# A two-layer transformer on one core: the retention layer laid out transposed, value weights centred once, gate by batch, head variance by a selector product, and a new order of all steps

## The chip, the cores and the metric

One core of a Trainium2 chip runs the whole program in one launch. The metric is the time on the device in microseconds, the median of three executions. TensorE (PE; its weight loads are shown as PEld) multiplies matrices, VectorE (DVE) and ScalarE (ACT) work on vectors and can read PSUM, GpSimd (POOL) works on SBUF alone, SyncE (SP) issues the DMAs.

## The reference

Two post-norm layers on 1024 rows of 256 channels (2 batches of 512). Layer 0 is retention with 8 heads of 32 channels and a ternary FFN; layer 1 is causal softmax attention with 16 heads of 16 and a mixture of experts (2 of 8, and a shared one). What the change touches is the retention:

```python
q, k, v, g = (x @ w + b for each)                 # w_v, w_g are 256 x 256
q, k = theta_shift(q), theta_shift(k)
sim = einsum('bhnd,bhsd->bhns', q, k / scale) * mask      # mask = gamma_h ** (n - s), 0 above
ret = einsum('bhns,bhsd->bhnd', sim, v)
r = (ret - mean) / sqrt(var + EPS)                # per row and head, over 32 channels
gate = silu(g) * (r * gn_weight + gn_bias)
return gate @ w_o + b_o                           # then x = layernorm(x + that)
```

The mean over a head's channels is linear in v. It is therefore the same to take it from each head's columns of w_v and b_v before anything is multiplied.

## The kernel before

Rows are handled in 8 tiles `t` of 128 (4 for each batch). Every weight and activation of the f16 products is split into a head and a rest ("split", L834 on ACT, L1001 on DVE), and one product is three matmuls per 128-deep slice (`cut_product`, L583; its bias matmul is L590). For tile t of the retention the steps are:

- `proj`: q, k, v and g in one product, two halves of 512 columns; ACT copies both halves out (L849, L850). `proj` on DVE (L1017) and POOL (L1240, L1241), then `rot` (L1024, L1025) rotate q and k.
- `tqk` (L623) transposes q and k, `sc` (L631) forms the scores, ACT copies them (L854), POOL masks them (L1247). `kv` (L638) adds to a running state, DVE L1033, L1035 and L1038.
- `ret`: state part L651, then one matmul for each head (L655), rows on the partitions. DVE computes mean, centring, square, sum and variance (L1048 to L1055). ACT computes the tanh of the gate (L877), POOL its products with the norm's weight and bias (L1258 to L1261) and then the power -1/2 (L1263).
- `gn`: three multiplies and adds on DVE (L1061 to L1065); `ty`: transpose (L662), split by ACT (L886) and DVE (L1069); `wo`: product and layer norm (L988 to L1081, with POOL's power in L1269); `tx`: transpose for the next stage (L678).

Later steps are `up`, `cut`, `dn` (FFN), `qk`, `tq`, `mx`, `tm`, `se`, `pv`, `ya` (attention; `pv`, L766, is a product with 32 output partitions for each of four heads) and `rt`, `rc`, `mu`, `mt`, `md` (experts).

All engines go through one list, SCHEDULE, and each issues its part of each step in that order. The list is made when the program is built. `schedule()` walks the dependences with the costs in COST and, among the steps that could start within SLACK of the earliest, takes the one with the longest remaining path plus its number in URGE (by kind) and NUDGE (by step). The same walk places steps in five PSUM tiles: three of 1024 columns (psum_a), two of 512 (psum_b). An engine executes strictly in its order, so a step that waits holds up all steps behind it on that engine. Layer 1 can start its `qk` only when all of the first retention is done (the memory is shared).

## Time and profile before

| what | value |
|---|---|
| median of 3 runs | 490.53 us (489.29 to 492.24) |
| the profiled execution, first to last instruction | 489.6 us |
| PE busy | 405.2 us, 83% |
| DVE, ACT, POOL busy | 314.7, 196.4, 141.8 us |
| mean granted PE clock | 0.897 of full speed |

The span leaves out what lies before the first and behind the last instruction of the profiled execution, for which the profile has no time. Its 489.6 us are 0.9 us below the median of the runs. Busy times of engines overlap. What counts is which engine the others wait for in each stretch.

### The profile page before, as it was taken

The page shows a single profiled execution, that of the slowest core. Times are in us where ns is not written, and L with a number is a line of the kernel's source. Part 1 is how long each engine was busy: PE and PEld are TensorE (multiplying, and loading weights), DVE is VectorE, ACT ScalarE, POOL GpSimd, SP SyncE. Part 2 cuts the span into 40 slices and gives each one's busy share as a digit, 9 for nine tenths or more (in the row PEclk, how much of TensorE's full clock was granted, in tenths as well). Part 3 has the DMA queues.
Part 4 walks back from the last instruction along what each step waited for, and adds up shares of the span by engine and source line. Part 5 has one row for each costly group of instructions (what it writes and reads, how often), then busy time and mean ns, then how long its engine had stood idle before and what let it go on. Part 6 is the DMA issues. An engine that isn't in the chain of part 4 may idle for free. (4 is left out here: it accounts for less than half of the span.)

```text
span 489.6 us, 7799 instructions
## 1 busy us (share of the span) xinstructions
PE 405.2 (83%) x2978; PEld 250.6 (51%) x2978; DVE 314.7 (64%) x689; ACT 196.4 (40%) x356; POOL 141.8 (29%) x182
## 2 busy tenths in 40 slices
PE   2697959568867876888889779998998989999996
PEld 0345646454634542323337334465565757767775
DVE  4547674794877679248438984445646887586554
ACT  4339543123323440588475114635534331241220
POOL 4458874843863000266320001212111000000000
PEclk9879578766989997699899757999999999999999
DMA  7912120200000000005000000000000000000000
GB/s 244 376 28 76 45 55 34 86 0 1 1 1 0 1 2 0 1 11 184 1 0 1 2 0 1 0 3 0 2 2 1 0 1 23 1 0 13 12 12 32
DMA packets 6856, 15.38 MB, mean 31 GB/s; under 512 B 610, under 2 KB 4002, under 8 KB 6818
## 3 DMA queue, kind: packets, MB, share of 16 engines
q1 hardware_dynamic: 6820, 14.89, 9.4%
q8 instruction: 24, 0.39, 0.3%
q14 instruction: 12, 0.10, 0.1%
HBM read 13.84 MB, written 1.05 MB: 30 GB/s over the span
## 5 line engine op out<-in xcount | busy, mean ns | idle before, releaser
L583 PE MATMUL psum_a<-cut_weights,x_transposed 128*128 128x352 f16 (+2 forms) x768 | 141.3, 338 | 12.9 <-DVE cut_weights L1001 8.7
L583 PEld LDWEIGHTS psum_a<-cut_weights,x_transposed 128*128 128x128 f16 x768 | 74.8, 101 | 69.5 <-issue 14.8
L1269 POOL TENSOR_TENSOR ln_rstd<-ln_var_eps,minus_half 128x1 f32<-128x1 f32 x32 | 23.7, 742 | 188.3 <-DVE ln_var_eps L992 188.3
L1286 POOL TENSOR_SCALAR_AFFINE_SELECT arena_mixers<-arena_mixers 128x256 f32<-128x256 f32 (+1 forms) x48 | 24.7, 517 | 108.6 <-ACT arena_mixers L936 108.6
L951 ACT ACTIVATE arena_ffn<-psum_a 128x352 f32<-128x352 f32 x48 | 22.3, 464 | 72.4 <-PE psum_a L583 72.4
L1145 DVE TENSOR_REDUCE arena_mixers<-psum_a 128x2 f16<-128x768 f32 (+3 forms) x44 | 47.3, 1124 | 1.4 <-PE psum_a L740 1.4
L936 ACT ACTIVATE arena_mixers<-psum_a 128x1024 f32<-128x1024 f32 (+2 forms) x48 | 42.0, 883 | 11.1 <-PE psum_a L756 5.7
L1184 DVE SCALAR_TENSOR_TENSOR arena_ffn<-arena_ffn,psum_a 128x352 f32<-128x352 f32 x48 | 24.9, 519 | 31.5 <-ACT arena_ffn L951 16.5
L583 PE MATMUL psum_b<-cut_weights,arena_ffn 128*128 128x256 f16 (+1 forms) x357 | 40.8, 273 | 0.0
L583 PEld LDWEIGHTS psum_b<-cut_weights,arena_ffn 128*128 128x128 f16 (+1 forms) x357 | 34.2, 98 | 5.9 <-issue 1.7
L1187 DVE SCALAR_TENSOR_TENSOR arena_ffn<-arena_ffn,router,psum_a 128x176 f32<-128x176 f32 (+1 forms) x80 | 31.9, 432 | 1.7
L766 PE MATMUL psum_b<-arena_mixers 128*32 128x512 f32 (+3 forms) x256 | 25.0, 463 | 7.9 <-POOL arena_mixers L1286 7.7
L988 DVE SCALAR_TENSOR_TENSOR z<-psum_b,residual 128x256 f32<-128x256 f32 x31 | 13.1, 421 | 26.7 <-PE psum_b L583 22.2
L694 PE MATMUL psum_a<-x_transposed,arena_ffn 128*128 128x512 f16 (+1 forms) x96 | 28.0, 444 | 1.3 <-DVE x_transposed L1089 1.3
L956 ACT ACTIVATE arena_ffn<-psum_a 128x1024 f16<-128x1024 f32 x16 | 16.4, 1026 | 26.9 <-PE psum_a L793 15.0
L1001 DVE SCALAR_TENSOR_TENSOR cut_weights<-stage,cut_weights 128x1024 f16<-128x1024 f32 (+3 forms) x19 | 22.9, 1208 | 5.5 <-ACT cut_weights L834 5.4
L1196 DVE TENSOR_TENSOR arena_ffn<-psum_a,arena_ffn 128x1024 f16<-128x1024 f32 x16 | 19.6, 1223 | 8.1 <-ACT arena_ffn L956 7.1
L890 ACT ACTIVATE x_transposed<-psum_b 128x256 f16<-128x256 f32 x24 | 9.3, 386 | 34.2 <-PE psum_b L678 34.0
L583 PE MATMUL psum_b<-cut_weights,y_transposed 128*128 128x256 f16 x96 | 14.9, 297 | 7.3 <-DVE y_transposed L1069 7.3
L1118 DVE SCALAR_TENSOR_TENSOR arena_ffn<-arena_ffn,psum_a 128x512 f32<-128x512 f32 (+1 forms) x12 | 8.2, 686 | 18.3 <-ACT arena_ffn L898 16.2
L756 PE MATMUL psum_a<-arena_mixers 64*128 64x512 f16 (+3 forms) x128 | 18.2, 315 | 1.8 <-ACT arena_mixers L928 1.8
L740 PE MATMUL psum_a<-arena_mixers 64*128 64x128 f16 (+3 forms) x128 | 19.6, 354 | 0.0
(159 smaller groups left out, 687.0 us busy)
## 6 DMA issues: line engine op xcount, KB each, us to landing
stage<-in_wup SPq DMA_DIRECT2D x8, 512.0 KB, 3.5
stage<-in_wdown SPq DMA_DIRECT2D x4, 512.0 KB, 4.6
arena_ffn<-in_w SPq DMA_DIRECT2D x1, 1408.0 KB, 10.4
stage<-in_xT SPq DMA_DIRECT2D x2, 512.0 KB, 4.4
stage<-in_wqkvg SPq DMA_DIRECT2D x2, 512.0 KB, 5.2
residual<-in_x SPq DMA_DIRECT2D x2, 512.0 KB, 9.1
out<-residual SPq DMA_DIRECT2D x8, 128.0 KB, 1.7
stage<-in_wqkv SPq DMA_DIRECT2D x2, 384.0 KB, 9.9
```

Of the source, the lines that this page charges most:

```text
L583: ins = mm(dst, lhs[k][a], rhs(k, b, col), start=(k == 0 and a == 0 and b == 0), stop=(bias_at is None and k == n - 1 and a == 1))
L694: ins = mm(ps[0:rows, gu, :], w, XT[:, a, k, n * TB * P:(n + 1) * TB * P], start=(k == 0 and a == 0), stop=(k == KD - 1 and a == 1))
L740: ins = mm(out_of[:, h % 2, h // 2, 0:(i + 1) * P], QT[r:r + 64, p, i * P:(i + 1) * P], KT[r:r + 64, p, 0:(i + 1) * P], start=False, stop= ...
L766: ins = mm(ps[32 * s:32 * s + 32, j * P:TB * P], V[:, b * TB + j, 4 * g + s, :], PE1[:, j % 2, s, 0:(TB - j) * P], start=(j == 0), stop=(j ...
L936: ins = nc.scalar.activation(heads, by_row_tile(ps, se_heads(j))[:, :, :, 0:w], ACT.Exp, scale=1.0 / 16)
L951: nc.scalar.activation(TG[:, n % 2, :], ps[:, 0, 0:MCW], ACT.Tanh, scale=0.5 * UN).then_inc(mu_tanh, 1)
L1001: v.scalar_tensor_tensor(rest, src, SA if PIECES[i][0] == "xT" else SW, head, ALU.mult, ALU.subtract).then_inc(rest_cut, 1)
L1145: v.tensor_reduce(ST[:, i, 0, h0:h0 + n_h, 48].rearrange("p (h s) -> p s h", s=2), by_row_tile(ps, n_h)[:, :, :, 0:(i + 1) * P], AX.X, ALU ...
L1184: link(v.scalar_tensor_tensor(AG[:, n % 2, :], TG[:, n % 2, :], 1.0, ps[:, 0, 0:MCW], ALU.add, ALU.mult))
L1187: ins = v.scalar_tensor_tensor(H[:, c * MCW + at:c * MCW + at + w], AG[:, n % 2, at:at + w], small[:, t % 2, 48 + e:49 + e], ps[:, 1, at:a ...
L1269: g_.tensor_tensor(rstd[:, r:r + 1], veps[:, r:r + 1], half[:, 0:1], ALU.pow).then_inc(ln_rstd[layer], 1)
L1286: g_.affine_select(out=part, in_=part, compare_op=ALU.is_ge, fill=0.0, base=0, pattern=[[0, se_heads(j)], [1, P]], channel_multiplier=-1). ...
```

## The change

Value weights are centred by head in the staging buffer, before they are split: step `cen` for pieces 1 and 2, with the bias row (new L1125 to L1132). The projection keeps q, k and v alone (512 and 256 columns). The gate is formed for a whole batch by `pg`, transposed: 12 matmuls of 512 columns (new L683), two ACT copies with the bias, one tanh of 1024 columns, one DVE instruction (new L1178). The decay is put wholly into the tables, so the state needs no decay factor. `ret` forms its output transposed, channels on the partitions, four heads in four groups of 32 output partitions (new L724). ACT squares it and copies it times the norm's weight (new L975, L977). `vr` sums the squares by head with a selector matmul (new L732), and DVE adds EPS, POOL takes the power, and ACT widens it to 256 columns (new L983). `rx` transposes that (new L739) and DVE multiplies (new L1192). `yg` adds the bias and multiplies by the gate (new L1202), `yh` splits the result (new L991, L1208), and `wo` follows without a transpose of y. `gn` and the layer-0 `ty` are gone. COST, SLACK, URGE and NUDGE have new numbers (NUDGE has 230 entries instead of 11). Excerpts:

```diff
     "split": "A1.07 D1.49", "bias": "A1.23 D1.39", "wsum": "A2.70", "gsum": "T0.07 D1.07", "quant": "D1.50",
-    "proj": "T3.18 A1.00 d0.73 p1.76", "rot": "D0.94", "tqk": "T1.17 A0.50", "sc": "T0.90 A0.50 p0.60",
-    "kv": "T0.49 D1.77", "ret": "T1.60 A0.30 D0.95 d0.80 p4.40", "gn": "D2.35", "ty": "T0.18 A0.30 D0.40",
+    "cen": "D1.15", "pg": "T2.60 A2.50 d1.20", "proj": "T2.25 A0.90 d0.73 p1.76", "rot": "D1.05", "tqk": "T0.60 A0.50",
+    "sc": "T0.90 A0.50 p0.60", "kv": "T0.49 D0.84", "ret": "T0.90 A1.12", "vr": "T0.40 D0.15 p1.80 a0.38",
+    "rx": "T0.25 D0.42", "yg": "D0.70", "yh": "A0.38 D0.45", "ty": "T0.18 A0.30 D0.40",
...
-SLACK = 0.789
+SLACK = 0.8987
...
+    ("split", 2): -71.9, ("mu", 2, 3): -87.8, ("proj", 5): 9.2, ("pv", 0, 3, 2): -1.3, ("yh", 7): 12.2,
...
+        if i in (1, 2):
+            add(("cen", i), at(i > 1, ("cen", 1)))
+        add(("split", i), at(i, ("split", i - 1)), at(i in (1, 2), ("cen", i)), at(i > LATE, pv_at(i - LATE - 1) if i - LATE - 1 < 16 else None))
+    add(("bias", 0), ("cen", 2))
...
+    for b in range(NB):
+        add(("pg", b), ("split", 3 if b else 2), at(b, ("pg", 0)))
...
-        add(("ret", t), ("sc", t, 0), ("sc", t, 1), at(i, ("kv", t - 1)), at(t > 1, ("gn", t - 2)))
-        add(("gn", t), ("ret", t), at(t > 1, ("ty", 0, t - 2)))
...
+        add(("ret", t), ("sc", t, 0), ("sc", t, 1), at(i, ("kv", t - 1)), at(t > 1, ("yg", t - 2)))
+        add(("vr", t), ("ret", t), at(t > 1, ("rx", t - 2)))
+        add(("rx", t), ("vr", t), at(t > 1, ("yh", t - 2)))
+        add(("yg", t), ("rx", t), ("pg", b))
+        add(("yh", t), ("yg", t), at(t > 1, ("wo", 0, t - 2)))
+        add(("wo", 0, t), ("yh", t), ("split", 4), at(t > 1, ("ln", 0, t - 2)))
...
-                    ins = cut_product([(ps[:, 0, :], 0), (ps[:, 1, :], 512)], x_tiles(t),
-                                      lambda k, b, c: w[:, b, k, c:c + 512], 0, None if t else weights)
+                    ins = cut_product([(ps[:, 0, :], 0), (ps[:, 1, 0:D], 512)], x_tiles(t),
+                                      lambda k, b, c: w[:, b, k, c:c + (D if c else 512)], 0, None if t else weights)
+                elif kind == "pg":
+                    b = step[1]
+                    pe.wait_ge(rest_cut, NTH[("split", 3 if b else 2)])
+                    claim(step)
+                    w = ws[:, :, W_QKVG:W_O0].rearrange("p a (k n) -> p a k n", k=KD)
+                    for g in range(KD):
+                        for k in range(KD):
+                            for a, c in ((0, 0), (0, 1), (1, 0)):
+                                ins = mm(ps[:, g, :], w[:, a, k, 3 * D + g * P:3 * D + (g + 1) * P],
...
-                            mm(ps[:, g * P:(g + 1) * P], QKT[:, t % 3, g, :], TS[:, c - 1, g * P:(g + 1) * P],
+                            mm(ps[:, g * P:(g + 1) * P], TS[:, c - 1, g * P:(g + 1) * P], QKT[:, t % 3, g, :],
                                start=(g == 0), stop=False, skip_group_check=True)
-                    for h in range(RH):
-                        g, s = divmod(h, 4)
-                        ins = mm(ps[:, h * RD:(h + 1) * RD], PT[:, t % 2, s // 2, s % 2, g, :],
-                                 VG[:, t % 4, h * RD:(h + 1) * RD],
-                                 start=(h == 0 and not c), stop=(h == RH - 1), skip_group_check=True)
+                    for g in range(2):
+                        for s in range(4):
+                            h = 4 * g + s
+                            ins = mm(ps[32 * s:32 * s + 32, g * P:(g + 1) * P], V0[:, t % 4, h * RD:(h + 1) * RD],
+                                     PT[:, t % 2, s // 2, s % 2, g, :], start=(g == 0 and not c), stop=(g == 1),
+                                     skip_group_check=True)
...
+                    for g in range(2):
+                        ins = mm(ps[:, 4 * g:4 * g + 4], SQ[:, t % 2, g * P:(g + 1) * P], con[:, C_HEAD:C_HEAD + P // RD],
+                                 start=(g == 0), stop=(g == 1), skip_group_check=True)
...
+                    for g in range(2):
+                        ins = nc.tensor.transpose(ps[:, g * P:(g + 1) * P], SQ[:, t % 2, g * P:(g + 1) * P], ident)
...
+                    if i in (1, 2):
+                        act.wait_ge(v_centred, i)
...
+                        act.wait_ge(v_centred, 3)
...
-                    nc.scalar.activation(VG[:, t % 4], ps[:, 1, :], ACT.Copy, scale=UN).then_inc(evac0, 1)
+                    nc.scalar.activation(V0[:, t % 4], ps[:, 1, 0:D], ACT.Copy, scale=UN).then_inc(evac0, 1)
...
+                    for g in range(KD):
+                        ins = nc.scalar.activation(SG[:, b, g, :], ps[:, g, :], ACT.Identity, scale=UN,
+                                                   bias=gate_col[:, 2 * KD + g:2 * KD + g + 1])
...
+                    nc.scalar.activation(TH[:, :, :].rearrange("p g t -> p (g t)"), SG[:, b].rearrange("p g t -> p (g t)"),
+                                         ACT.Tanh, scale=0.5).then_inc(tanh0, 1)
...
+                    nc.scalar.activation(SQ[:, t % 2, :], ps[:, 0:D], ACT.Square)
+                    for g in range(KD):
+                        ins = nc.scalar.activation(RT[:, t % 2, g * P:(g + 1) * P], ps[:, g * P:(g + 1) * P], ACT.Copy,
+                                                   scale=gate_col[:, g:g + 1])
...
+                    nc.scalar.activation(SQ[:, t % 2, :].rearrange("p (h d) -> p h d", h=RH),
+                                         head_rstd[:, t % 2].unsqueeze(2).to_broadcast([P, RH, RD]), ACT.Copy)\
...
+                    nc.scalar.activation(YT[:, t % 2, 0, :], Y[:, t % 2, :], ACT.Copy, scale=0.5 * SA).then_inc(y0_head, 1)
...
+                    i = step[1]
+                    dve.wait_ge(piece_in[i], 16)
+                    parts = [(P, stage[:, i % NSTAGE, 2 * D:3 * D], v_sum[:, i - 1])]
+                    if i == 2:
+                        dve.wait_ge(bias_in, 16)
+                        parts.append((2, bias_raw[0:2, 2 * D:3 * D], v_sum[0:2, 2]))
+                    for _, w, total in parts:
+                        ins = v.tensor_reduce(total, w.rearrange("p (h d) -> p h d", h=RH), AX.X, ALU.add)
+                    link(ins)
...
+                    for rows, w, total in parts:
+                        heads = w.rearrange("p (h d) -> p h d", h=RH)
+                        v.tensor_tensor(heads, heads, total.unsqueeze(2).to_broadcast([rows, RH, RD]), ALU.add)\
+                            .then_inc(v_centred, 1)
...
+                    if t >= 2:
+                        dve.wait_ge(pe_done, PLACE[("tqk", t - 2)][3])
+                        if (t - 2) % TB < TB - 1:
+                            dve.wait_ge(pe_done, PLACE[("kv", t - 2)][3])
...
                         link(v.tensor_tensor(KVM, ps[:, 0:D], block_g, ALU.mult))
-                        for g in range(2):
-                            w = slice(g * P, (g + 1) * P)
-                            ins = v.scalar_tensor_tensor(TS[:, c, w], TS[:, c - 1, w], con[:, C_G128 + g:C_G128 + g + 1],
-                                                         KVM[:, w], ALU.mult, ALU.add)
-                        ins.then_inc(state, 1)
+                        v.tensor_tensor(TS[:, c], KVM, TS[:, c - 1], ALU.add).then_inc(state, 1)
...
+                    v.scalar_tensor_tensor(SG[:, b].rearrange("p g t -> p (g t)"), TH[:, :, :].rearrange("p g t -> p (g t)"),
...
+                    v.tensor_scalar(head_var[:, t % 2], ps[:, 0:RH], EPS, None, ALU.add).then_inc(gvar, 1)
...
+                    v.tensor_tensor(Y[:, t % 2, :], RT[:, t % 2, :], ps[:, 0:D], ALU.mult).then_inc(rstd_read, 1)
...
+                    for g in range(KD):
+                        y = Y[:, t % 2, g * P:(g + 1) * P]
+                        ins = v.scalar_tensor_tensor(y, y, gate_col[:, KD + g:KD + g + 1], SG[:, b, g, i * P:(i + 1) * P],
+                                                     ALU.add, ALU.mult)
...
+                    v.scalar_tensor_tensor(YT[:, t % 2, 1, :], Y[:, t % 2, :], 0.5 * SA, YT[:, t % 2, 0, :],
+                                           ALU.mult, ALU.subtract).then_inc(y0_rest, 1)
...
-                    link(g_.tensor_tensor(GC[:, t % 2], TH[:, t % 2], gate, ALU.mult))
-                    link(g_.tensor_tensor(GC[:, t % 2], GC[:, t % 2], gate, ALU.add))
-                    link(g_.tensor_tensor(GA[:, t % 2], GC[:, t % 2], gnorm[:, 0:D], ALU.mult))
-                    g_.tensor_tensor(GC[:, t % 2], GC[:, t % 2], gnorm[:, D:2 * D], ALU.mult).then_inc(gates, 1)
...
+                    g_.tensor_tensor(head_rstd[:, t % 2], head_var[:, t % 2], half[:, 0:RH], ALU.pow).then_inc(grstd, 1)
...
-        own = gammas[4 * g + part // RD] ** P
-        block[:, g * P:(g + 1) * P] = own[:, None] * (part[:, None] // RD == part[None, :] // RD)
-        con[:, C_G128 + g] = own
+        block[:, g * P:(g + 1) * P] = part[:, None] // RD == part[None, :] // RD
...
+    con[:, C_HEAD:C_TOT] = (part[:, None] // RD == np.arange(P // RD)[None, :]) / RD
```

First place: DVE's first instructions, from the first split to the second half of the weights. Before:

```order
L1001 SCALAR_TENSOR_TENSOR x_transposed<-stage,x_transposed 128x2x512
L1001 SCALAR_TENSOR_TENSOR cut_weights<-stage,cut_weights 128x1024
L1008 SCALAR_TENSOR_TENSOR bias_rows<-arena_mixers,constants,bias_rows 2x1280
L1001 SCALAR_TENSOR_TENSOR cut_weights<-stage,cut_weights 128x1024
L1001 SCALAR_TENSOR_TENSOR x_transposed<-stage,x_transposed 128x2x512
```

The same engine and place of the changed kernel:

```order
L1115 SCALAR_TENSOR_TENSOR x_transposed<-stage,x_transposed 128x2x512
L1125 TENSOR_REDUCE arena_mixers<-stage 128x8
L1128 TENSOR_SCALAR arena_mixers<-arena_mixers 128x8
L1132 TENSOR_TENSOR stage<-stage,arena_mixers 128x256
L1125 TENSOR_REDUCE arena_mixers<-stage 128x8
L1125 TENSOR_REDUCE arena_mixers<-arena_mixers 2x8
L1128 TENSOR_SCALAR arena_mixers<-arena_mixers 128x8
L1128 TENSOR_SCALAR arena_mixers<-arena_mixers 2x8
L1132 TENSOR_TENSOR stage<-stage,arena_mixers 128x256
L1132 TENSOR_TENSOR arena_mixers<-arena_mixers 2x256
L1115 SCALAR_TENSOR_TENSOR cut_weights<-stage,cut_weights 128x1024
L1139 SCALAR_TENSOR_TENSOR bias_rows<-arena_mixers,constants,bias_rows 2x1024
```

Nine centring instructions now stand ahead of the first split of a weight, for which PE's first matmul waits.

Second place: DVE again, a little later, up to the first rotation (L1024 and L1025 before, L1161 and L1162 after) and what follows it. Before:

```order
L1017 TENSOR_TENSOR arena_mixers<-arena_mixers 128x512
L1001 SCALAR_TENSOR_TENSOR cut_weights<-stage,cut_weights 128x1024
L1024 TENSOR_TENSOR arena_mixers<-arena_mixers 128x16x16
L1025 TENSOR_TENSOR arena_mixers<-arena_mixers 128x16x16
L1017 TENSOR_TENSOR arena_mixers<-arena_mixers 128x512
L1033 TENSOR_TENSOR arena_mixers<-psum_b,arena_mixers 128x256
```

The changed kernel, from the first L1150 (the old L1017) on:

```order
L1150 TENSOR_TENSOR arena_mixers<-arena_mixers 128x512
L1178 SCALAR_TENSOR_TENSOR arena_mixers<-arena_mixers 128x1024
L1150 TENSOR_TENSOR arena_mixers<-arena_mixers 128x512
L1115 SCALAR_TENSOR_TENSOR cut_weights<-stage,cut_weights 128x1024
L1178 SCALAR_TENSOR_TENSOR arena_mixers<-arena_mixers 128x1024
L1115 SCALAR_TENSOR_TENSOR cut_weights<-stage,cut_weights 128x768
L1139 SCALAR_TENSOR_TENSOR bias_rows<-arena_mixers,constants,bias_rows 2x1024
L1115 SCALAR_TENSOR_TENSOR cut_weights<-stage,cut_weights 128x768
L1161 TENSOR_TENSOR arena_mixers<-arena_mixers 128x16x16
L1162 TENSOR_TENSOR arena_mixers<-arena_mixers 128x16x16
```

Both gates (L1178), the splits of pieces 5 and 6 (128x768, the weights of layer 1's attention) and the second bias row moved ahead of the first rotation.

Third place: PE at a tile of the retention with its state part. Before (L662 transposes y, L651 and L655 are `ret`, then `wo`):

```order
L662 MATMUL psum_b<-constants,y 128x128 x2
L651 MATMUL psum_b<-arena_mixers 128x128 x2
L655 MATMUL psum_b<-arena_mixers 128x32 x8
L583 MATMUL psum_b<-cut_weights,y_transposed 128x256 x6
L590 MATMUL psum_b<-bias_rows,constants 128x256
```

The changed kernel (L719 and L724 are `ret`, L739 `rx`, L706 `kv`, L732 `vr`, L691 `tqk`):

```order
L739 MATMUL psum_b<-constants,arena_mixers 128x128 x2
L691 MATMUL psum_b<-constants,arena_mixers 128x128 x4
L719 MATMUL psum_a<-arena_mixers 128x128 x2
L724 MATMUL psum_a<-arena_mixers 32x128 x8
L706 MATMUL psum_b<-arena_mixers 128x128 x2
L732 MATMUL psum_b<-constants,arena_mixers 128x4 x2
```

The eight matmuls of a head each have 128 columns and 32 output partitions instead of 32 columns and 128 output partitions. Two matmuls of four columns are new.

## Rows read from the trace of the kernel before

**Rows 1.** The page: busy times, and PE's clock and DMA in 40 slices.

```profile
PE 405.2 (83%) x2978; PEld 250.6 (51%) x2978; DVE 314.7 (64%) x689; ACT 196.4 (40%) x356; POOL 141.8 (29%) x182
...
PEclk9879578766989997699899757999999999999999
DMA  7912120200000000005000000000000000000000
```

**Rows 2.** Windows by stage: length; busy PE, PEld, DVE, ACT, POOL; clock; DMA.

```profile
8.40:35.00 26.60, 21.43 (x90) 10.37 (x91) 13.68 (x17) 9.73 (x15) 14.32 (x15) 0.81 0.62 214
35.00:60.00 25.00, 21.37 (x133) 14.45 (x132) 19.15 (x40) 18.47 (x30) 22.13 (x23) 0.81 0.21 61
60.00:87.00 27.00, 21.74 (x136) 14.21 (x133) 16.61 (x35) 9.97 (x18) 16.43 (x18) 0.80 0.14 43
87.00:114.20 27.20, 15.11 (x85) 12.96 (x83) 23.55 (x46) 5.92 (x13) 17.10 (x18) 0.64 0.13 39
114.20:145.80 31.60, 25.61 (x144) 14.92 (x144) 20.86 (x47) 10.88 (x22) 19.29 (x21) 0.87 0.01 1
145.80:151.70 5.90, 3.96 (x28) 2.42 (x28) 4.58 (x17) 0.90 (x3) 1.52 (x4) 1.00 0.00 0
151.70:199.50 47.80, 35.29 (x314) 20.72 (x314) 36.55 (x54) 15.87 (x33) 3.45 (x5) 0.91 0.00 1
...
295.50:405.00 109.50, 101.34 (x790) 61.83 (x791) 66.05 (x189) 48.09 (x93) 15.47 (x31) 0.98 0.01 1
405.00:489.60 84.60, 79.98 (x641) 60.91 (x638) 52.25 (x142) 20.45 (x44) 3.89 (x7) 0.99 0.04 13
```

**Rows 3.** Waits of PE: us in total, times, the longest.

```profile
PE psum_b L662 <- DVE y L1065: 9.8, 5, 5.4
...
PE psum_b L623 <- DVE arena_mixers L1025: 7.8, 3, 4.2
...
PE psum_b L638 <- DVE arena_mixers L1025: 3.5, 1, 3.5
```

**Rows 4.** Timeline of the opening: start, us, instruction, idle before it.

```profile
5.84 1.23 DVE L1001 SCALAR_TENSOR_TENSOR x_transposed<-stage,x_transposed 128x1024 f16<-128x1024 f32 x1 [5.84 <-ACT x_transposed L834]
...
8.47 2.72 PE L583 MATMUL psum_a<-cut_weights,x_transposed 128*128 128x512 f16 x6 [8.47 <-DVE cut_weights L1001]
...
18.79 0.85 DVE L1024 TENSOR_TENSOR arena_mixers<-arena_mixers 128x256 f32<-128x256 f32 x1
```

**Rows 5.** Timeline of PE at its upper clock: start, us, instructions.

```profile
83.24 2.76 PE L583 MATMUL psum_a<-cut_weights,x_transposed 128*128 128x512 f16 x12
...
130.26 1.87 PE L655 MATMUL psum_b<-arena_mixers 128*128 128x32 f32 x16
...
151.76 2.13 PE L583 MATMUL psum_a<-cut_weights,x_transposed 128*128 128x512 f16 x12 [0.71 <-DVE x_transposed L1089]
153.72 0.49 PE L590 MATMUL psum_a<-bias_rows,constants 128*128 128x512 f16 x2
...
334.08 0.42 PE L766 MATMUL psum_b<-arena_mixers 128*32 128x128 f32 x8
```

**Rows 6.** Groups by form: busy us, mean ns of one, idle before.

```profile
L1263 POOL TENSOR_TENSOR arena_mixers<-arena_mixers,minus_half 128x8 f32<-128x8 f32 x8 | 15.9, 1990 | 2.9 <-DVE arena_mixers L1055 2.9
...
L1259 POOL TENSOR_TENSOR arena_mixers<-arena_mixers 128x256 f32<-128x256 f32 x8 | 6.0, 756 | 0.6
...
L1064 DVE TENSOR_TENSOR y<-y,arena_mixers 128x256 f32<-128x256 f32 x8 | 5.5, 688 | 0.3
...
L1038 DVE SCALAR_TENSOR_TENSOR arena_mixers<-arena_mixers,constants 128x128 f32<-128x128 f32 x8 | 4.7, 630 | 0.1
...
L877 ACT ACTIVATE arena_mixers<-arena_mixers 128x256 f32<-128x256 f32 x8 | 3.3, 410 | 0.0
...
L1048 DVE TENSOR_REDUCE arena_mixers<-psum_b 128x8 f32<-128x256 f32 x6 | 2.5, 422 | 2.3 <-PE psum_b L655 2.2
L1055 DVE TENSOR_SCALAR arena_mixers<-arena_mixers 128x8 f32<-128x8 f32 x8 | 1.4, 171 | 0.3
```

233 lines of the change are left out of this document (134 added, 99 removed), and 44 rows, old and new, of the table NUDGE.

## The prediction

> **What bounds the kernel now.** I read the page's busy line and its slices first, then the span cut into stages, then the waits, and last the durations by form. The busy line has PE in front with 83% of the span, then DVE with 64% [rows 1]. That average hides two halves. From 295.5 us on, PE is busy for 101.34 of 109.5 us and for 79.98 of 84.6 us at a clock of 0.98 and 0.99 [rows 2]. There PE's own work is the bound, and none of that work is changed. From 8.4 to 151.7 us, where the retention and the first half of the FFN run, it is different. The six windows up to 151.7 add up to 143.3 us with 109.2 us of PE busy, thus 34.1 us idle, and the clock is 0.64 to 0.87 in five of them [rows 2]. The reader should see two losses there: PE waits, and because it waits it works for long stretches at the lower of its two levels (1.2 instead of 2.4 GHz). For what PE waits is in the waits: for the y of the group norm (9.8 us) and for DVE's rotation (7.8 and 3.5 us), 21.1 us together [rows 3]. DVE and POOL are not full in that stretch either (98.4 and 90.8 us of 143.3 [rows 2]), but both are in the chain of a tile, one after the other. In the third and fourth windows of it POOL has 16.43 and 17.10 us of 27 [rows 2]. So the bound of the stretch is a chain through DVE, POOL and PE with PE's work as the largest part. Between 151.7 and 199.5 us DVE with 36.55 of 47.8 us leads [rows 2], by the row maxima, which stay.
>
> **The change part by part, PE.** All at the upper clock. The projection is 12 matmuls of 512 columns (2.76 us) and two of bias. The new one has the form that layer 1's has now, six of 512 and six of 256, 2.13 us [rows 5]. Its two bias matmuls took 0.49 us there [rows 5]; the old two of 512 columns cost about 0.1 us more, an estimate from the ratio of the twelve. The saving is 0.63 + 0.1 = 0.7 us for each of 8 tiles, 5.8 us. The gate by batch adds 2 times 12 matmuls of 512 columns, 2 x 2.76 = 5.5 us [rows 5]. The two cancel. The within-tile product was 16 records of 32 columns, 1.87 us. The new one is two groups of the form with four column groups, of which one took 0.42 us for 8 records [rows 5], thus 0.84 us. It saves 1.03 x 8 = 8.2 us. The selector matmul adds 4 records in which the weight load is all, 1.87/16 x 4 = 0.47 us, 3.7 us over 8 tiles. The transpose `rx` takes the place of `ty`. Sum: -5.8 + 5.5 - 8.2 + 3.7 = -4.8 us at the upper clock. Over the stretch the mean clock is 0.80, so about -6 us of busy time. That is what the stretch is worth if nothing but PE's work counted.
>
> On that form a rule of the Trainium skill speaks against the change. The row has eight weight loads and eight matmuls of one row group within 0.42 us [rows 5], 0.05 us each, so the four column groups do run side by side. The page "TensorE: Matmul & The Clock Gate", section "The mechanism", says that a weight load overlaps running matmuls only when its row group differs, and here all four share it. By that rule the loads stand in line as they do now, `ret` saves nothing, and the sum for PE is +3.4 us in place of -4.8. The trace disagrees with the rule; I go by the row and keep the rule as a small rival.
>
> **DVE.** Gone for each tile are eight full-width instructions (reduce, centre, square, reduce, three of `gn`, the rest of y). One of these takes from 0.42 us (L1048) to 0.69 us (L1064), and I take 0.53, the middle. With two small ones of at least 0.17 us [rows 6] that is 4.6 us. New are two full-width ones (0.42 each), two of 128 columns, and one small one. A row with that form has 0.63 us (L1038) [rows 6], probably with waiting in it, so 0.21 (half of L1048) to 0.63; I take 0.5. That is 2.0 us. Net -2.6 x 8 = -21 us. The state saves about 0.8 us on 4 tiles. The centring adds three reduces, three small ones and three additions, 6 x 0.42 + 3 x 0.17 = 3.0 us, and the gates take 2 x 1.23 (the form of the split [rows 4]). So -21 - 3 + 3 + 2.5 = -18.5 us, between -9 and -33 by the ends.
>
> **POOL and ACT.** POOL loses four multiplies of 0.76 us for each tile [rows 6], 24 us, and keeps the power (1.99 us each). ACT loses a tanh of 0.41 us for each tile and half a copy of v (0.2), and gets a square, two scaled copies of half the width and a widening of about 0.4, 0.5 and 0.41 us (L877 is the measure [rows 6]). Each batch adds two copies of 512 columns and a tanh of 1024, at 0.41 us for 256 columns 3.3 us. In sum +0.7 x 8 + 2 x 3.3 = +12 us. ACT is busy for 55.9 us of the 143 [rows 2], so I cost this at nothing. The cover is ACT's idle time. If it is gone, each tile's chain grows by the 1.3 us of square, copies and widening.
>
> **The chain of a tile.** From the product to `wo` it was six DVE instructions, the power, three DVE, transpose, ACT, DVE. Now it is ACT three times, PE, DVE, POOL, ACT, PE, DVE three times, ACT, DVE. By the same rows both are 7 to 8 us, so I count no gain in latency. The gain is in what is queued beside it: on POOL, masks, rotations and powers no longer stand behind 3 us of gate products, and on DVE a rotation waits behind 2.0 us less for each tile. These are the queues in front of PE's 21.1 us of waits [rows 3]. I take back half of it, 10 us; the ends are 3 (only queues of POOL shrink) and 18. With fewer waits, the window 87.0 to 114.2 (clock 0.64, PE busy 15.11) comes nearer to the 0.80 of its neighbours [rows 2]: 15.11 x (1 - 0.64/0.80) = 3 us; ends 0 and 8 (all six windows at 0.9).
>
> **The opening.** Here the change adds waits. PE's first matmul waits for the first split weight at 8.47 us [rows 4]. The centring of both pieces stands ahead of it on DVE: 6 x 0.42 + 3 x 0.17 = 3.0 us, ending about 10.3. The ACT half of the split waits for the centring of its own piece too, and the DVE half follows. PE starts at about 11.6, +3 us. Queued behind it on DVE are the bias row and both other splits, for which PE's second half of tile 0 waits, so the shift stays. SP's load of piece 4 waits for the same split and goes out 3 us later; nobody waits for it then. Second, the first rotation was at 18.8 us [rows 4]. Now both gates and pieces 5 and 6 stand ahead of it. DMA is busy to about 25 us (slices of 12.2 us with 7, 9, 1 tenths [rows 1]), so the pieces are no hindrance before that. But the second gate waits for four groups of matmuls on PE: 11.6 + two projections and two gates, which end near 27 to 29. Then follow ACT and four DVE instructions of 1.2 us each. The rotation comes near 34 us. PE has tile 2's projection in hand, then waits some 4 to 8 us. As against this, splits, bias row and a weight sum that stood later are done. I count +3 and +3, ends +1 and +13.
>
> **Sum.** -6 (PE's work) -10 (waits) -3 (clock) +6 (opening) = -13 us in the first 152 us. Behind it no work of PE changes, and the new order can win or lose; the waiting that is left from 295.5 us on is 8.2 + 4.6 us [rows 2]. I count -2, within -6 and +6. The profiled execution spans 489.6 us, the median of the runs is 0.9 above. 490.5 - 15 = 475.5, so **475.5 us**.
>
> **Rivals.** (a) The work is smaller, but the first rotations come so late that most is given back. For: the 15 us by which the first rotation moves. Against: PE has work that it needs anyway. -6 - 5 + 0 + 7 = -4, 486 us, and with the tail's -2 484. The page's rule above would end in the same place: 475.5 + 8.2 = 484. (b) The order of the first half, freed of POOL and DVE, lets PE run nearly dense: -6, -18, -8, +3 and -2, 460 us. For: in the windows of the tail it does [rows 2]. Against: its chain of a tile is no shorter. (c) Slower. The place is the first tile: PE starts 3 us late, idles until the rotation at 34 or more, falls to its lower level, and the 12 us that ACT gets stand in each tile's chain (1.3 x 8 = 10 us), since ACT's copies for the scores queue behind them. +13 + 10 - 6 - 5 = +12, 502 us; it decides when ACT's share in the stretch passes that of PE. Against: ACT has 61% of that stretch free. (d) The order behind 295.5 us, where PE is full, loses 8 to 13 us by new gaps, and the result is within 0.5% of before: nothing to see, 490 us.
>
> **How the numbers follow.** Forecast (467 to 483) 0.54; (a) 0.18, of it 0.03 for the page's rule; (b) 0.12; (d) 0.08; (c) 0.08. Half a per cent is about what a measurement of this kernel can tell from no change. Faster by more: 0.54 + 0.17 + 0.12 = 0.83. Within: 0.01 + 0.08 = 0.09. Slower: 0.08. The range leaves out (c), half of (b) and part of (d): 461 to 489. The forecast's own range is 467 to 483.
>
> **What would show it.** Right: the first matmul at 11 to 12 us; the first rotation at 30 to 36 us; the new `ret` at 0.8 to 1.0 us of PE for its eight heads at the upper clock; POOL's busy time down by 20 to 28 us and DVE's by 9 to 33; layer 1's first `qk` at about 137 to 140 us instead of 151.76; the stretch from the first expert product to the end as long as before within 6 us. Wrong: if `qk` starts no earlier although PE's work is smaller, the opening has eaten it (a, c). If it starts 12 us earlier and the end does not, it is (d). If the eight heads take 1.9 us, the page was right.

## The result, and the profile after

The changed kernel takes 466.63 us (median of 4 runs, 466.61 to 466.66), the kernel before 491.24 us beside it. The ratio is 0.951, with a 95% interval of 0.9475 to 0.9545. All medians here leave out executions in a second, slow state (among the kernels of the experiments one of e7, 656.85 us, and one of e10, 1988.16 us). The profiled execution spans 464.9 us, 24.7 less than before. The page, in answer to [rows 1]:

```profile
span 464.9 us, 7904 instructions
PE 394.7 (85%) x3034; PEld 243.1 (52%) x3034; DVE 295.4 (64%) x656; ACT 204.4 (44%) x386; POOL 110.2 (24%) x150
PEclk9977889889959865899998579999999999999999
DMA  7940000133000000122000000000000000000001
```

PE has 10.5 us less than before, DVE 19.3 and POOL 31.6 us less, ACT 8.0 us more. The span is best divided in two, at layer 1's first `qk`. The columns are those of [rows 2]. The kernel before, up to that point and behind it:

```profile
8.47:151.76 143.29, 109.21 (x611) 69.30 (x611) 98.42 (x198) 55.81 (x99) 90.77 (x96) 0.80 0.21 66
151.76:489.60 337.84, 295.95 (x2368) 181.30 (x2368) 213.71 (x490) 135.75 (x253) 48.41 (x79) 0.94 0.04 11
```

The changed kernel:

```profile
11.57:137.10 125.53, 101.19 (x694) 63.18 (x695) 79.14 (x164) 64.47 (x130) 59.11 (x63) 0.86 0.22 70
137.10:464.90 327.80, 293.49 (x2341) 179.93 (x2339) 210.79 (x482) 135.29 (x252) 47.67 (x77) 0.93 0.04 12
```

The front, from PE's first matmul on, is 17.8 us shorter: PE has 8.0 us less work in it and is idle for 24.3 instead of 34.1 us. It starts 3.1 us later, so the first `qk` comes 14.7 us earlier. The back is 10.0 us shorter, although the change leaves its work as it was. In the front two of the eight `dn` products more are done (48 of 96 records instead of 24), so the two parts are not quite the same work; 24 such records took 3.1 us of PE in the front of the kernel before. The first expert product came at 275.5 us instead of 297.1. So the back falls into a first part of 138.4 us, 6.9 shorter, and a last part of 189.4 us, 3.1 shorter; both have almost the same PE work as before, but PE is idle for 23.1 instead of 29.7 us in the first part:

```profile
137.10:275.54 138.44, 115.33 (x919) 57.80 (x917) 91.12 (x149) 68.05 (x118) 28.47 (x39) 0.83 0.06 18
```

```profile
151.76:297.14 145.38, 115.66 (x944) 59.09 (x944) 96.06 (x165) 68.52 (x121) 29.59 (x42) 0.87 0.06 17
```

The first of these rows is the changed kernel's, the second that of the kernel before.

For what PE waits in the front of the changed kernel (in answer to [rows 3]; us, times, the longest):

```profile
PE psum_a L640 <- DVE cut_weights L1115: 11.9, 2, 11.6
PE psum_b L691 <- DVE arena_mixers L1162: 8.1, 4, 5.1
PE psum_b L640 <- DVE y_transposed L1208: 4.7, 4, 2.2
PE psum_b L760 <- DVE residual L1226: 3.1, 2, 2.3
PE psum_b L739 <- ACT arena_mixers L983: 1.6, 1, 1.6
```

The wait for the group norm's y (9.8 us before) is gone with its step. What is left is the start and the rotation, 5.1 of its 8.1 us for the first one. The opening, in answer to [rows 4]:

```profile
11.57 2.08 PE L640 MATMUL psum_a<-cut_weights,x_transposed 128*128 128x512 f16 x6 [11.57 <-DVE cut_weights L1115]
...
30.77 0.41 DVE L1161 TENSOR_TENSOR arena_mixers<-arena_mixers 128x256 f32<-128x256 f32 x1
...
31.56 1.12 PE L691 MATMUL psum_b<-constants,arena_mixers 128*128 128x128 f32 x4 [5.14 <-DVE arena_mixers L1162]
```

PE's new forms, in answer to [rows 5] (`pg`, `ret`, and `vr` at the lower level of the clock):

```profile
16.50 2.78 PE L683 MATMUL psum_a<-x_transposed,cut_weights 128*128 128x512 f16 x12
...
42.89 0.65 PE L724 MATMUL psum_b<-arena_mixers 128*32 128x128 f32 x16
...
44.56 1.02 PE L732 MATMUL psum_b<-constants,arena_mixers 128*128 128x4 f32 x4 [0.17 <-ACT arena_mixers L977]
```

And by form, in answer to [rows 6]:

```profile
L1400 POOL TENSOR_TENSOR arena_mixers<-arena_mixers,minus_half 128x8 f32<-128x8 f32 x8 | 13.3, 1662 | 4.7 <-DVE arena_mixers L1185 4.5
...
L1202 DVE SCALAR_TENSOR_TENSOR y<-y,arena_mixers 128x128 f32<-128x128 f32 x16 | 7.8, 526 | 0.1
...
L983 ACT ACTIVATE arena_mixers<-arena_mixers 128x256 f32<-128x256 f32 x8 | 3.3, 417 | 27.6 <-POOL arena_mixers L1400 27.6
```

ACT stands still for 27.6 us behind POOL's powers; the price of that is seen only where somebody waits for ACT.

### The profile page after: what moved, and what is told of

It reads as the page before. It is cut to its first block, busy times and chain, and to the rows that moved or that the text cites. A ratio compares the mean times of both kernels' runs of the same rounds, so it can differ in the third digit from the quotient of the medians.

```text
span 464.9 us, 7904 instructions
## 1 busy us (share of the span) xinstructions
PE 394.7 (85%) x3034; PEld 243.1 (52%) x3034; DVE 295.4 (64%) x656; ACT 204.4 (44%) x386; POOL 110.2 (24%) x150
## 4 chain that ended last, share of the span: by engine, by line
PE 58%; DVE 22%; ACT 9%; issue 6%; POOL 4%; DMA 1%; POOLq 0%; DVEq 0%
PE psum_a L640 24%; PE psum_b L640 10%; DVE arena_mixers L1290 8%; PE psum_a L776 5%; PE psum_b L848 3%; ACT arena_mixers L1050 2%; PE psum_a L838 2%; PE psum_a L880 1%; DVE arena_ffn L1332 1%; PE psum_b L830 1%; PE psum_a L875 1%; PE psum_a L647 1%; PE psum_b L788 1%; PE psum_b L760 1%; DVE arena_ffn L1329 1%
## 5 line engine op out<-in xcount | busy, mean ns | idle before, releaser
L640 PE MATMUL psum_a<-cut_weights,x_transposed 128*128 128x352 f16 (+3 forms) x774 | 134.9, 327 | 13.3 <-DVE cut_weights L1115 11.9
L1406 POOL TENSOR_TENSOR ln_rstd<-ln_var_eps,minus_half 128x1 f32<-128x1 f32 x32 | 19.7, 615 | 196.6 <-DVE ln_var_eps L1106 196.6
L640 PE MATMUL psum_b<-cut_weights,arena_ffn 128*128 128x256 f16 (+1 forms) x408 | 46.7, 273 | 0.0
L640 PEld LDWEIGHTS psum_b<-cut_weights,arena_ffn 128*128 128x128 f16 (+1 forms) x408 | 39.1, 98 | 6.8 <-issue 1.7
L848 PE MATMUL psum_b<-arena_mixers 128*32 128x512 f32 (+3 forms) x256 | 23.7, 444 | 8.3 <-POOL arena_mixers L1423 8.3
L1042 ACT ACTIVATE arena_mixers<-psum_b 128x1024 f16<-128x1024 f16 x7 | 7.2, 1026 | 39.6 <-PE psum_b L830 39.6
L1070 ACT ACTIVATE arena_ffn<-psum_a 128x1024 f16<-128x1024 f32 x16 | 16.4, 1024 | 16.8 <-PE psum_a L880 13.3
L1263 DVE SCALAR_TENSOR_TENSOR arena_ffn<-arena_ffn,psum_a 128x512 f32<-128x512 f32 (+1 forms) x12 | 8.2, 684 | 20.1 <-ACT arena_ffn L1012 11.2
L822 PE MATMUL psum_a<-arena_mixers 64*128 64x128 f16 (+3 forms) x128 | 20.6, 369 | 0.0
L819 PE MATMUL psum_a<-constants 128*128 128x128 f16 x128 | 17.1, 248 | 3.1 <-DVE arena_mixers L1290 2.7
L1150 DVE TENSOR_TENSOR arena_mixers<-arena_mixers 128x512 f32<-128x512 f32 x8 | 6.1, 759 | 21.2 <-ACT arena_mixers L932 21.2
```

Source lines behind the costliest of these rows:

```text
L640: ins = mm(dst, lhs[k][a], rhs(k, b, col), start=(k == 0 and a == 0 and b == 0), stop=(bias_at is None and k == n - 1 and a == 1))
L822: ins = mm(out_of[:, h % 2, h // 2, 0:(i + 1) * P], QT[r:r + 64, p, i * P:(i + 1) * P], KT[r:r + 64, p, 0:(i + 1) * P], start=False, stop= ...
L848: ins = mm(ps[32 * s:32 * s + 32, j * P:TB * P], V[:, b * TB + j, 4 * g + s, :], PE1[:, j % 2, s, 0:(TB - j) * P], start=(j == 0), stop=(j ...
L1406: g_.tensor_tensor(rstd[:, r:r + 1], veps[:, r:r + 1], half[:, 0:1], ALU.pow).then_inc(ln_rstd[layer], 1)
```

## Experiments

The theory of the prediction was: PE's smaller work and the emptier queues of DVE and POOL shorten the front, the order brings almost nothing. The rival that grew out of the result: the order brings it. Each window row below ends or starts at the first `qk` of its kernel; "front" is the stretch from the first matmul to it, "back" the rest.

**The order by itself: e1, e10, e11.** In e1 the changed kernel's list is made with the numbers of before.

```diff
-SLACK = 0.8987
+SLACK = 0.789
```

URGE and NUDGE are exchanged in the same way (their lines are left out here).

> The changed kernel with SLACK, URGE and NUDGE of the kernel before (costs and steps of the new layer, the kinds cen, pg, vr, rx, yg, yh without a number). It splits the layer from the searched order. Theory A (the layer's smaller work and the emptier queues of DVE and POOL bring most of it, the search the rest): 472 to 480 us, layer 1's first qk at 137 to 145 us. Theory B (the searched numbers are what brings it, the new layer only changes what there is to order): 484 to 492 us, with the first qk behind 148 us. Theory C (the layer alone; the numbers bring nothing): 465 to 469 us.

Measured: 509.04 us, ratio 1.0351 (1.0274 to 1.0427). All three expectations missed, B by the least; 12.9 us of the loss stand behind the first `qk` (350.7 us in place of 337.8), where the change leaves the work as it was. But numbers that were chosen for other steps give an accidental order, so e10 carries the order itself over: the list is given, and the walk only places the steps in PSUM. The old order has no place for the new steps; they were put in by hand, `vr` right behind `ret` in all eight tiles, `rx` and `yg` where `gn` stood.

```diff
+ORDER = [('split', 0), ('cen', 1), ('cen', 2), ('split', 1), ('bias', 0), ('split', 2), ('split', 3),
...
-        start, step, tile = max((x for x in best if x[0] <= first + SLACK), key=...)
+        start, step, tile = next(x for x in best if x[1] == ORDER[len(order)])
```

> The changed kernel's layer in the order of the kernel before, step for step: vr stands right behind ret, rx and yg where gn stood, yh where the transpose of y stood, the centring ahead of the first split of a weight, each pg behind a projection of its batch. So the layer's work changes and the order does not. Theory A (the smaller work of PE, DVE and POOL counts by itself; e1 was slow because old numbers make an accidental order of new steps): 478 to 486 us, the first qk at 140 to 147 us. Theory B (the new chain of a tile has more hops between engines than the old one, and an order made for the old one waits for them): 490 to 505 us, with PE waiting for POOL's power or ACT's widening (rx behind vr) for 10 us and more.

Measured: 494.57 us, ratio 1.007 (1.0032 to 1.0107). Theory B. The front and the back of e10:

```profile
11.44:153.22 141.78, 105.04 (x666) 64.70 (x666) 77.03 (x156) 65.30 (x129) 60.57 (x62) 0.79 0.19 62
153.22:492.60 339.38, 299.40 (x2368) 181.64 (x2368) 213.83 (x490) 135.88 (x253) 48.51 (x79) 0.92 0.04 11
```

The work did fall as in the changed kernel (DVE by 21, POOL by 30, PE by 4 us in the front), and the first `qk` came 1.5 us later than before. PE's idle time in the front went up from 34.1 to 36.7 us. Where it went is seen at `vr` and `rx`, in the list of PE's waits:

```profile
PE psum_b L801 <- ACT arena_mixers L1046: 8.3, 7, 2.2
PE psum_b L808 <- ACT arena_mixers L1052: 5.0, 3, 2.4
```

L801 is `vr`, which waits for ACT's square of `ret`; L808 is `rx`, which waits for ACT's widening. What PE and its weight loads together waited for at `vr`, in e10:

```profile
L801 PE MATMUL psum_b<-constants,arena_mixers x32: 244/253/373, 36.4 to 134.1; 128*128 128x4 f32 x32
its engine sat idle before it (us, times) until:
  ACT arena_mixers L1046: 20.6, 15
```

and in the changed kernel:

```profile
L732 PE MATMUL psum_b<-constants,arena_mixers x32: 172/253/376, 44.6 to 128.8; 128*128 128x4 f32 x32
its engine sat idle before it (us, times) until:
  ACT arena_mixers L977: 2.5, 6
```

`vr` cannot start before ACT has squared what `ret` gave. Right behind `ret` it makes PE stand still in seven of the eight tiles, for 1.2 us on average (8.3 us in all). In the changed kernel at least one other step of PE stands between the two in every tile, and the same wait is 0.9 us in all. (The two rows above add the waits of PE and of its weight loads, which overlap.) The waits at `vr` and `rx` are 13.3 us together, and they hang on where the new steps were put. A run with the old order and `vr` one step later was not made. So e10 shows that the new layer wins nothing with this placement, not that it wins nothing in any version of the old order. e11 is the mirror: the kernel before with the changed kernel's list as ORDER, and with its waits of DVE in `proj` and `rot`.

```diff
+                    if t >= 2:
+                        dve.wait_ge(rotated, t - 1)
...
+                    if t >= 2:
+                        dve.wait_ge(pe_done, PLACE[("tqk", t - 2)][3])
```

> The kernel before in the order of the changed kernel, step for step: its gn stands where yg stands, its first transpose of y where yh stands; the centring, pg, vr and rx have no counterpart. Its rotation gets the waits of the changed kernel. It fills the fourth field beside before (old layer, old order, 491), the changed kernel (new, new, 467) and e10 (new layer, old order, 495). If the order is worth the same with either layer (additive, 28 us by e10 against the changed kernel): 463 to 470 us. If the gain needs both (the order can place the new layer's short steps and has nothing to win with the long ones on DVE and POOL): 484 to 500 us. I hold the second likelier, since e5 and e6 showed that this order bears no load on POOL or DVE.

Measured: 509.18 us, ratio 1.0375 (1.0317 to 1.0433), slower than both cases I wrote down. Its front and back:

```profile
8.76:177.96 169.20, 124.40 (x638) 78.85 (x639) 97.07 (x206) 55.37 (x100) 89.64 (x97) 0.73 0.17 55
177.96:506.10 328.14, 291.13 (x2341) 179.17 (x2339) 210.60 (x482) 135.38 (x252) 47.72 (x77) 0.94 0.04 12
```

with, among PE's waits:

```profile
PE psum_b L690 <- DVE arena_mixers L1098: 14.0, 4, 7.9
PE psum_b L729 <- DVE y L1138: 13.1, 5, 3.9
```

In the kernel before these two waits, for the rotation at the transposes and for the group norm's y, were 7.8 and 9.8 us [rows 3]. So the four corners, in us of the median, are:

| | order of before | order of after |
|---|---|---|
| layer of before | 491.2 | 509.2 |
| layer of after | 494.6 | 466.6 |

The new layer alone (with `vr` right behind `ret`) costs 3, the new order alone 18, both together win 25. The way I read it, and no run shows it by itself: the new order leaves each tile's norm only the room that the short steps need, and the new steps need others between them. The first half rests on e5, e6 and e11 (more work in this order costs a lot), the second on the two rows of `vr`.

**The back: e2, e3.** e2 is the changed kernel up to `wo` of the last tile, then the order of before; e3 the kernel before up to that step, then the order of after (both with an ORDER list as in e10).

> The changed kernel with its own order up to the last product of the first retention, wo(0,7), and from there on the steps in the order of the kernel before. Theory A (the 10 us gained behind the first qk come from the new order there): first qk at 137 us as before, the end near 476 us. Theory D (they are left over from the front, since two FFN products more are done before the first qk, and the rest falls in place): 466 to 469 us.

> The kernel before with its own order up to wo(0,7), and from there on the steps in the order of the changed kernel. The mirror of e2. Theory A: the new order behind brings 6 to 10 us here too, 481 to 485 us, the first qk at 150 to 152 us. Theory D: 489 to 492 us; the FFN products come ahead of the first qk, so it starts later, but nothing is won.

Measured: e2 476.98 us (ratio 0.9707, 0.9661 to 0.9753), e3 487.69 us (0.9931, 0.9901 to 0.9961). The back of e2, then of e3:

```profile
139.00:475.60 336.60, 294.62 (x2339) 179.99 (x2337) 208.55 (x476) 134.95 (x251) 46.58 (x76) 0.93 0.04 11
```

```profile
157.91:487.50 329.59, 292.02 (x2341) 179.61 (x2339) 210.06 (x479) 135.37 (x253) 45.10 (x74) 0.93 0.04 12
```

e2 has the same four `dn` in its front as the changed kernel and still needs 336.6 us behind it. So theory A holds for e2: behind the new front the new order of the back is worth 8.8 us (10.4 in the medians, where the stretch up to the first `qk` has changed too), 7.7 of it as PE's idle time (42.0 us in e2, 34.3 in the changed kernel). e3 came out between its two cases. Its back is short too (329.6), but 3.9 of the 8.2 us are PE work that has moved ahead of `qk` with the two extra `dn`, and the front is 6.1 us longer. Idle time in the back fell by 4.3 us, that in the front rose by 1.7. So with the old layer the same exchange is worth 3.7 us in the medians. In every run except e1 the back takes 336.6 to 339.4 us in the old order and 326.5 to 330.8 us in the new one.

**What load on each engine costs: e5, e6, e7, e9.** e5 is the first piece of the diff (POOL, step `vr`), e6 the second (DVE, step `rx`).

```diff
+                    pool.wait_ge(ret_copied, t + 1)
+                    for _ in range(4):
+                        link(g_.tensor_tensor(load[:, 1], load[:, 0], load[:, 0], ALU.mult))
...
+                    for _ in range(4):
+                        link(v.tensor_tensor(load[:, 1], load[:, 0], load[:, 0], ALU.mult))
```

> The changed kernel with four more multiplies of 240 columns on POOL for each tile of the retention, in a row ahead of the power, where the gate products stood before (their result is not used). That gives POOL back about 8 x 4 x 0.7 = 22 us. Queue theory (the relief of POOL was a good part of the 9 us of PE waits that went): 4 to 12 us slower than the changed kernel, 471 to 479 us, the powers later. Rival (POOL had room enough, its relief is worth nothing): 466 to 468 us.

> The changed kernel with four more multiplies of 240 columns on DVE for each tile, in a row ahead of rx (their result is not used): 8 x 4 x 0.4 to 0.5 = 13 to 16 us more for DVE, of the 19 that it lost. Queue theory: DVE is in every step of a tile, so it costs more than POOL's load by the us: 6 to 14 us slower, 473 to 481 us. Rival (DVE has 46 us of 126 idle before the first qk, the load goes there): 466 to 469 us.

Measured: e5 482.97 us (ratio 0.9849, 0.9784 to 0.9913), e6 489.94 us (0.9976, 0.9943 to 1.0009). The fronts of e5 and of e6:

```profile
11.51:155.02 143.51, 111.12 (x695) 69.11 (x695) 81.56 (x164) 64.57 (x130) 80.85 (x95) 0.78 0.19 61
```

```profile
11.51:157.71 146.20, 110.61 (x694) 69.51 (x695) 93.65 (x196) 65.38 (x130) 59.76 (x63) 0.78 0.19 60
```

POOL's 21.7 us more lengthen the front by 18.0 us, DVE's 14.5 us more by 20.7 us, and both medians lie above what the queue theory gave. The clock falls from 0.86 to 0.78, so PE's own time grows by 10 us as well. One caution: in e5 the load waits for `ret` to be copied, so it stands in the chain of a tile, while the old gate products could run beside DVE's mean and variance. It is an upper price, and what the order has to do with it is not parted from that. The same engine relieved in the old order is e9: the kernel before without its four gate products on POOL (the gate is left out of the result).

> The kernel before without POOL's four gate products for each tile (the gate is left out of the result, y is the normalized value); all else and the order as it was. It takes 24 us from POOL and nothing else. Queue theory as in the prediction (POOL's queue held the chain of a tile): 5 to 10 us faster, 481 to 486 us. Rival (in this order POOL is late only because the engines before it are): 489 to 492 us.

Measured: 486.42 us, ratio 0.9898 (0.9844 to 0.9951). Its front:

```profile
8.63:146.03 137.40, 106.05 (x611) 66.80 (x611) 93.71 (x198) 55.29 (x99) 64.55 (x64) 0.84 0.21 69
```

The front ends 5.7 us earlier for 26.2 us less on POOL, and PE is idle for 31.4 instead of 34.1 us in it: the queue theory, at its low end. Relief of POOL alone does help in the old order. e7 gives work to PE instead.

```diff
-                            ins = mm(ps[32 * s:32 * s + 32, g * P:(g + 1) * P], V0[:, t % 4, h * RD:(h + 1) * RD],
+                            ins = mm(ps[:, g * P:(g + 1) * P], V0[:, t % 4, g * P:(g + 1) * P],
```

> The changed kernel with each head's product in ret over all 128 output partitions (128 columns of weights) instead of 32, so that no two of the four heads can run side by side; the sums then mix heads, all else is the same. Theory A (the four column groups run side by side, that is why 16 records take 0.65 us): 16 records in 1.6 to 2.6 us, PE busy 8 to 15 us more, and 6 to 14 us slower, 473 to 481 us. By the rule of the Trainium skill, page "TensorE: Matmul & The Clock Gate", section "The mechanism", a weight load overlaps a running matmul only if its row group differs; all row groups are the same in both kernels, so by it the records would take as long here as in the changed kernel, and the time would stay within 2 us of 466.6.

Measured: 467.32 us (three executions, 465.12 to 469.76), ratio 0.9512 (0.9426 to 0.9598). The changed kernel has 466.63 us and a ratio of 0.951, so the runs do not tell the two apart. The profiled execution is the slowest of the three, its span 3.1 us above that of the changed kernel. Its first `ret`, its weight loads and its front:

```profile
43.01 2.05 PE L724 MATMUL psum_b<-arena_mixers 128*128 128x128 f32 x16
```

```profile
L724 PEld LDWEIGHTS psum_b<-arena_mixers x96: 186/192/338, 43.0 to 123.0; 128*128 128x128 f32 x96
```

```profile
11.59:141.46 129.87, 106.82 (x694) 72.36 (x695) 78.25 (x164) 64.64 (x130) 59.88 (x63) 0.90 0.21 67
```

Theory A is right on the records (about 1.95 us for 16 in place of 0.65; over the eight tiles 16.8 instead of 5.6 us of PE) and wrong on the time. The expectation drawn from the page was wrong on the records and had the time right (within 2 us of 466.6), for a reason that it did not give. Of 11.2 us more for `ret`, only 5.6 remain in PE's busy time of the front, where the granted clock is 0.90 instead of 0.86, and only 4.3 in its length.

**The opening: e8, e4, e12.** Here the differences to the changed kernel are near what the intervals resolve, and the profiled spans, 464.9 against 460.5 and 459.4 us, are read beside the medians. e8 leaves out the centring (the mean stays in the result).

```diff
-                    if i in (1, 2):
-                        act.wait_ge(v_centred, i)
...
-                    for _, w, total in parts:
-                        ins = v.tensor_reduce(total, w.rearrange("p (h d) -> p h d", h=RH), AX.X, ALU.add)
...
```

> The changed kernel without the centring of the value weights (the nine DVE instructions and ACT's waits for them are gone, the mean stays in the result). It prices the opening: the first matmul at 8.4 to 8.9 us instead of 11.57. If the shift stays to the end: 463 to 464 us. If the gap before the first rotation takes it up: 466 to 467 us, with PE's wait there as long as before or longer.

Measured: 463.32 us, ratio 0.9431 (0.938 to 0.9483). The first matmul came at 9.14 us, 2.4 earlier, and the first `qk` at 132.84, 4.3 earlier. The profiled span is 4.4 us shorter, so the shift stays to the end. e4 changes the first 34 steps. In short form (these are not lines of the file), the changed kernel has

> proj 0, pg 0, proj 1, split 4, pg 1, split 5, bias 1, split 6, wsum 0, rot 0, proj 2, tqk 0, kv 0, ...

and e4 has

> proj 0, rot 0, pg 0, proj 1, tqk 0, kv 0, rot 1, sc 0, pg 1, split 4, proj 2, ..., split 5, ...

> The changed kernel with the first 34 steps in another order: the rotation of tile 0 stands right behind its projection and ahead of both gates, that of tile 1 ahead of the second gate, the splits of pieces 5 and 6 and the second bias row come later; everything behind is as in the changed kernel. Theory A (the late first rotation is a loss of the opening: PE waits 5.1 us for it and 1.75 us for the third one): first rotation at 20 to 21 us, the wait gone, 461 to 464 us. Rival (PE has to do that work at some time and DVE's splits are only moved to where they are waited for): 465.5 to 468 us.

Measured: 462.15 us, ratio 0.9431 (0.9383 to 0.948), 4.5 us below the changed kernel, and the front ends at 132.79 us. From e4's timeline:

```profile
18.87 0.77 DVE L1230 TENSOR_TENSOR arena_mixers<-arena_mixers 128x256 f32<-128x256 f32 x1 [1.38 <-POOL arena_mixers L1456]
```

```profile
40.80 1.01 PE L801 MATMUL psum_b<-constants,arena_mixers 128*128 128x4 f32 x4 [3.61 <-ACT arena_mixers L1046]
```

The rotation is 11.9 us earlier and PE's wait of 5.1 us is gone. A new one of 3.6 us came up at the first `vr`, behind ACT's weight sum. e12 takes the sum out of its way.

> The changed kernel with e4's early rotation, and further with ret(0) and vr(0) ahead of the split of piece 6 and of the first weight sum, the second bias row and the second weight sum a few steps later. In e4 PE waited 3.6 us for ACT's copy of ret(0) behind that sum. Expected if that wait was a loss to the end: 457 to 460 us. If it is found elsewhere again (the weight sums then stand ahead of something else that PE waits for): 461 to 464 us as e4.

Measured: 463.79 us (ratio 0.9437, 0.9389 to 0.9484), the first `qk` at 135.25 us. The wait at the first `vr` fell to 0.5 us, others came in its place (2.2 us for ACT's copy of a projection), and the time did not improve on e4. e4 and e12 are not told apart by their intervals. All four times of e4 and five of the six of e12 lie below those of the changed kernel, but their intervals overlap its interval (0.9475 to 0.9545), so a gain of about 4 us is likely and not shown beyond doubt.

## Why the prediction was right or wrong

The direction held, and so did the wide range, 461 to 489. The forecast's own range, 467 to 483, was missed by a hair, and the time of 466.6 lies nearer to rival (b)'s 460 than to 475.5: 24.6 us won instead of 15. Of the 9 us between, 8 come from the term behind the first `qk`. In the front the sum came out well (-13 forecast, -14.7 measured), in part by luck, as its terms show:

- **PE's work, -6 us, and clock, -3 us.** Both end in PE's busy time, -9 together. The front shows -8.0, with two `dn` more in it, thus about -11 for like work. `ret` fell further than I took from the row: 0.65 us for eight heads instead of 0.84, against 1.87 before. But its worth was taken one for one, and that was wrong: e7 gives 11.2 us of such work back and loses 0.7 us in the medians, less than they resolve (4.3 in the front of the profiled execution). The granted clock was 0.80 before and 0.86 after, in e10 0.79 with more idle time. So it follows the waits, as the prediction had it, but not them alone: in e7 it is 0.90 with nearly the same idle time (23.1 us) as in the changed kernel.
- **Waits, -10 us**, less the 3 us that the late rotation was to add. The idle time of the front fell by 9.8 us. The size was about right and the reason only half: I put it down to emptier queues in whatever order. Emptier queues do help, e9 shows that for POOL (5.7 us). But e10 has the emptier queues and 2.6 us more idle time, and 13.3 us of its waits stand at the new steps behind ACT. I had the new hops between engines counted as "no gain in latency"; what I did not see is that on PE `vr` waits for ACT right behind `ret`, so that the place of the neighbours decides.
- **Opening, +6 us.** First matmul 11.57 us and PE's idle time before the first rotation 5.1 us, as said. e8 and e4 price both halves: 3.3 and 4.5 us of the medians, each near what the intervals resolve.
- **Behind the first `qk`, -2 us.** This is the term that was mis-sized. It measured -10.0, 3 us of which may be the work of the two `dn` that moved ahead of the first `qk`. I argued from PE's idle time behind 295.5 us alone, 12.8 us; another 29.1 us lay between 151.8 and 295.5 us, in a stretch that I had read for its DVE share. The sign that I gave held: from the first expert product to the end it is 3.1 us shorter. The other 6.9 us came ahead of it, where I had looked for nothing. e2 shows that the order made 8.8 us, with the same four `dn` ahead of the first `qk`. Why it leaves less idle time stays open.
- **DVE -18.5, POOL -24, ACT +12 us.** Measured -19.3, -31.6 (the four products made 25.4 of it; the powers took 1.66 instead of 1.99 us, 2.6 together, and those of the layer norms, which nobody changed, 4.0 less) and +8.0. That ACT costs nothing was about right in the order of after, where PE's waits for its answers at `vr` and `rx` are 2.5 us, and wrong in e10.
- **Rivals.** (c), slower by the chain through ACT, did not happen here, but something like its mechanism is what e10 shows: PE's waits for ACT's steps in each tile's chain used up the gain. (d) had the sign of the back wrong. (b) forecast a denser front, with waits down by 18 us and the clock at 0.9; they fell by 9.8, and the clock was 0.86. The rival that was missing is that the back gains by the order, and that layer and order can each lose alone.
- **The rule of the Trainium skill** (page "TensorE: Matmul & The Clock Gate", section "The mechanism"), by which loads overlap matmuls only in another row group; the same section also names loads into a background weight buffer as pulled ahead, which the prediction left out. All row groups are the same here. The records of 16 loads of 32 columns are 0.110 us each, 1.76 us in a row, within a `ret` of 0.65 us; so the records lie beside each other and beside those of matmuls. The prediction would have given the page right at 1.9 us for the eight heads; they take 0.65. The trace does not agree with the rule in its narrow form, and no run here shows whether the buffer is the reason. The load records themselves shrank with the width, from 0.192 us in e7 to 0.110 us. Neither the prediction's 1.9 us by the rule nor the expectation of e7 by it took that into account.

What stays open: which of the some 220 new numbers in NUDGE make the 9 us of the back, since only its whole order was exchanged. Open too is what the new layer would win in the old order with `vr` and `rx` placed better.

## What to carry to other kernels

When a change rewrites a stage and its order at once, carry the old order over to the new stage step for step and time that: here the new stage was worth nothing in it as its steps were placed, and the new order was worth less than nothing with the old stage. The steps that have no counterpart need care in such a run: in e10, 13.3 us of PE's waits stood at two of them. Where a step waits for another engine's answer to the step just before it, put other work between the two before counting what it saves. And price a saving by the engine that is waited for: in the tight new order a microsecond of POOL or DVE in the chain of a tile cost up to 0.8 or 1.4 us of the front, one of PE's own work 0.4, and in the old order one of POOL 0.2.
